# SyncE holds four loads back behind the first context, and seven tile norms move into the even rounds

## The chip, the cores and the metric

One core of a Trainium2 chip runs one launch of the kernel. The metric is the time of that launch on the device in microseconds (us). The engines are TensorE (PE, with its weight loads as PEld), VectorE (DVE), ScalarE (ACT), GpSimd (POOL) and SyncE (SP), which here only issues DMAs. Each runs its own instructions in order and waits on semaphores for the others.

## The reference

A small perceiver of six residual layers over `x` (16 sequences of 64 rows, 256 wide) and a context (16 x 1601 rows, 192 wide). The change touches only the first layer:

```python
x = x + _L0_xattn_ref(_layernorm(x), ctx_768, wq, bq, wk, bk, wv, bv, wo, bo)
# _L0_xattn_ref: 16 heads of 16
q = (x @ wq + bq)                      # from the normed x
k, v = (y @ wk + bk), (y @ wv + bv)    # from the context
attn = softmax(einsum('bqhd,bkhd->bhqk', q, k) / sqrt(16))
out = einsum('bhqk,bkhd->bqhd', attn, v) @ wo + bo
```

Self-attention, a feed-forward layer, a second cross-attention, a test-time-trained memory and a mixture of experts follow.

## The kernel before

The first layer is the function `latents`. `x` lies as 8 tiles of 128 rows (`c.x`, each tile two sequences). An item n (0 to 31) is one sequence and one half of the heads; b = n // 2 is the sequence. After a lead-in the layer runs rounds r from -3 to 64, two rounds an item. Each engine has its own function (`pe`, `dve`, `act`, `pool`, `sp`) which walks through the same rounds, so the place of a step in each of these lists is the order in which that engine does it.

What the rounds hold, as far as it is needed here:
- Context loads: `sp` loads the first context in two parts, columns 0 to 400 and the rest, three DMAs each; then `wq`, `wo`, the other seven tiles of `x`, the second context (`load_raw(1)`), the output bias `biasb` and two stores of zeros. `load_raw(2)` then waits for the split of the first context. ACT and POOL split every context into high and low parts (`split`, L689 and L690, L783 and L787; for the first context POOL L837 and DVE L648).
- PE, in a round from 0 on: `scores` of one group (4 banks of PSUM), `look_at` of one group (4 banks), `values` of the round before (1 bank), then a second `scores` (4 banks) and a second `look_at` (4 banks); after that in odd rounds the turn of the maxima, and in both kinds `keys` (L410 to L414) and `vals` (L425 to L429) for what comes next. Banks are given out by a counter modulo 8 (`at`), so the last of the four banks of the second `scores` is the one that the first `look_at` filled first, and the first three banks of the second `look_at` are the next three of it. PE waits for each (`take`) until it has been emptied.
- DVE empties the look banks with `maxima`, four TENSOR_REDUCE (L574) a group. In an even round it does: maxima, an add (L600), maxima, the maximum (L582 to L587), `invert` (L609), an add (L603). In an odd one: maxima, two adds (L603), maxima, `gather` (L617, L621), an add (L603).
- POOL in an even round: an add (L808), `blockdiag` (L797), two adds (L813), `scale` (L825, L828), then a split (L783, L787). In an odd round: adds (L813), a sum (L818), a split.
- The layer norm of a tile has three steps: `moments` on DVE (L169, L171), `root_pool` on POOL (L178 to L189, six tiny instructions that each wait for the one before), `norm_tile` on DVE (L196), which waits for the root. Tile 0 is done in the lead-in. `norms = {-3: (1, 2, 3), -2: (4, 5), -1: (6, 7)}` says in which round the others are: `moments` at the start of DVE's round, `root_pool` on POOL after `scale` and ahead of the split, `norm_tile` at the end of DVE's round, ahead of the next round's maxima. PE turns tile t (`turn_h`) in round 2t - 1.
- POOL adds the output bias to all of `c.x` in one instruction (L857) in round -1. DVE needs it in `project`, first in round 10.
- `dve_ahead` (L1091 to L1094) is a little work for the next layer, at the end of DVE's round 2.

Of the kernel before, what the change touches and what calls it, by code (L numbers as in the profile page):

```python
# [9 lines left out]
ALU = mybir.AluOpType  # L10
# [4 lines left out]
NT = 8  # L15
# [184 lines left out]
def latents(c, first, then):  # L200
# [30 lines left out]
    x0 = "x0"  # L231
# [6 lines left out]
    seen, m_made, m_turned, m_out = c.sig("seen"), c.sig("m_made"), c.sig("m_turned"), c.sig("m_out")  # L238
    added_d, added_p, totals = c.sig("added_d"), c.sig("added_p"), c.sig("totals")
    padded, in_ctx, in_rest = c.sig("padded"), (c.in_ctx, c.sig("in_ctx_odd")), c.sig("in_ctx_rest")  # L240
    norms = {-3: (1, 2, 3), -2: (4, 5), -1: (6, 7)}

    def probs(n, s):

# [108 lines left out]
    def sp(e, w):  # L353
        x = d["x"].rearrange("(t b) n c -> (b n) t c", b=2)
        for k in ("wk", "wv"):
            e.dma_start(W[k], d["x0_" + k]).then_inc(c.in_wkv.at(k, 16), 16)
        e.dma_start(c.x[:, 0, :], x[:, 0, :]).then_inc(c.in_wkv.at("x", 16), 16)
        for k, arrived in ((slice(0, 400), in_ctx[0]), (slice(400, NK), in_rest)):
            e.dma_start(raw1[0][:, k], d["ctxT"][0, 0:128, k]).then_inc(arrived.at(None, 16), 16)
            e.dma_start(raw2[0][0:64, k], d["ctxT"][0, 128:192, k]).then_inc(arrived.at(None, 16), 16)  # L360
            e.dma_start(raw2[0][64:128, k], d["ctxT"][0, 128:192, k]).then_inc(arrived.at((x0, 0), 16), 16)
            if k.start == 0:
                e.dma_start(c.ident[:, :], d["ident"]).then_inc(c.in_const.at("ident", 16), 16)
                e.dma_start(c.small[:, 0:c.n_const], d["small"]).then_inc(c.in_const.at("small", 16), 16)
        for k in ("wq", "wo"):
            e.dma_start(W[k], d["x0_" + k]).then_inc(c.in_wqo.at(k, 16), 16)
        e.dma_start(c.x[:, 1:NT, :], x[:, 1:NT, :]).then_inc(c.in_x.at("x", 16), 16)

        def load_raw(b):
            if b >= 2:  # L370
                w.wait_ge(*c.split_hi((x0, b - 2, 3)))
                w.wait_ge(*c.split_lo((x0, b - 2, 3)))
            if b == 2:
                w.wait_ge(*c.dv(("first low", 3)))
            e.dma_start(raw1[b % 2], d["ctxT"][b, 0:128, :]).then_inc(in_ctx[b % 2].at(None, 16), 16)
            e.dma_start(raw2[b % 2][0:64, :], d["ctxT"][b, 128:192, :]).then_inc(in_ctx[b % 2].at(None, 16), 16)
            e.dma_start(raw2[b % 2][64:128, :], d["ctxT"][b, 128:192, :]).then_inc(in_ctx[b % 2].at((x0, b), 16), 16)

        load_raw(1)
        e.dma_start(c.biasb[:, :], d["x0_bo"].partition_broadcast(128)).then_inc(c.in_bias[0].at("in", 16), 16)  # L380
        w.wait_ge(*c.po("zeros"))
        for v in (c.xs_d, c.ys_d):
            e.dma_start(v[1024:1152, :], c.zeros[:, :]).then_inc(c.zeroed.at("rows", 16), 16)
        for b in range(2, NB):
            load_raw(b)

    def pe(e, w):
# [53 lines left out]

        def queries(tile):
            w.wait_ge(*c.hT_act((x0, tile)))
            w.wait_ge(*c.in_wqo("wo"))
            bk = take("q", tile)
            for g in range(2):
                a = mm(e, ps[:, bk, 128 * g:128 * g + 128],
                       [(W["wq"][:, k, 128 * g:128 * g + 128], hT[:, k, 128 * tile:128 * tile + 128]) for k in range(2)])
            a.then_inc(c.q_made.at((x0, tile)), 1)
            emptied[bk] = c.q_out((x0, tile))  # L450
# [69 lines left out]

        def project(tile):
            w.wait_ge(*c.o_norm((x0, 4 * tile + 3)))
            bk = take("o", tile)
            mm(e, ps[:, bk, 0:256], [(aT[:, g, :], W["wo"][:, g, :]) for g in range(2)]).then_inc(c.projected.at((x0, tile)), 1)
            emptied[bk] = c.x_new((x0, tile))
# [34 lines left out]
    def dve(e, w):  # L560
# [61 lines left out]

        def project(tile):
            w.wait_ge(*c.projected((x0, tile)))
            w.wait_ge(*c.biased(x0))
            e.tensor_tensor(c.x[:, tile, :], ps[:, at("o", tile), 0:256], c.x[:, tile, :], ALU.add).then_inc(c.x_new.at((x0, tile)), 1)
            w.wait_ge(*c.x_new((x0, tile)))
            moments(c, e, w, x0, tile)
# [150 lines left out]
    def pool(e, w):  # L779
        def split(b, i):  # L780
            k = slice(400 * i, 400 * i + 400 + (i == 3))
            w.wait_ge(*c.split_hi((x0, b, i, 1)))
            e.tensor_tensor(c1l[b % 2][:, k], raw1[b % 2][:, k], c1h[b % 2][:, k], ALU.subtract).then_inc(c.po.at(), 1)  # L783
            w.wait_ge(*c.split_hi((x0, b, i)))
            w.wait_ge(*c.po.now())
            lo = c2[b % 2][64:128, k]
            e.tensor_tensor(lo, raw2[b % 2][64:128, k], lo, ALU.subtract).then_inc(c.split_lo.at((x0, b, i)), 1)  # L787
            w.wait_ge(*c.split_lo((x0, b, i)))

        def blockdiag(n):  # L790
            b, g = n // 2, n % 2
            w.wait_ge(*c.q_out((x0, b // 2)))
            w.wait_ge(*c.in_const("small"))
            if n >= 3:
                w.wait_ge(*c.scored((x0, n - 3, 3)))
            q = qT[b // 2 % 2][:, g, 64 * (b % 2):64 * (b % 2) + 64]
            e.tensor_tensor(qd[n % 3], q.unsqueeze(1).broadcast_to([128, 2, 64]), c.parq.unsqueeze(2).broadcast_to([128, 2, 64]),  # L797
                            ALU.mult).then_inc(c.q_diag.at((x0, n)), 1)

        def add(n, s):  # L800
            if (n, s) > (N - 2, 1):
                return
            v = probs(n, s)
            w.wait_ge(*c.exp_a((x0, n, s, 3)))
            if s == 0:
                if n:
                    w.wait_ge(*totals(n - 1))
                e.tensor_tensor(sums_p, v[:, :, 256:384], v[:, :, 384:512], ALU.add).then_inc(added_p.at((n, s)), 1)  # L808
            else:
                for t in range(share(n, s), GN[s]):  # L810
                    k = 128 if G0[s] + t < 12 else KL
                    w.wait_ge(*added_p.now())
                    e.tensor_tensor(sums_p[0:k], sums_p[0:k], v[0:k, :, 128 * t:128 * t + 128], ALU.add).then_inc(added_p.at((n, s)), 1)  # L813

        def add_both(n):
            w.wait_ge(*added_d((n, 3)))
            w.wait_ge(*added_p((n, 3)))
            e.tensor_tensor(sums_p, sums_p, sums_d, ALU.add).then_inc(added_p.at((n, "all")), 1)  # L818

        def scale(n):  # L820

            w.wait_ge(*c.o_out((x0, 2 * n + 1)))
            if n:
                w.wait_ge(*c.o_norm((x0, n - 1)))
            e.tensor_tensor(oS, va, vb[:, 0:128], ALU.add).then_inc(c.po.at(), 1)  # L825
            w.wait_ge(*c.po.now())
            w.wait_ge(*c.dv(("inverted", n)))
            e.tensor_tensor(oS, oS, rS, ALU.mult).then_inc(c.po.at(("scaled", n)), 1)  # L828

        e.memset(c.half, -0.5).then_inc(c.po.at("half"), 1)  # L830
        e.memset(c.eps, 1e-5).then_inc(c.po.at("eps"), 1)
        e.memset(c.zeros[:, :], 0.0).then_inc(c.po.at("zeros"), 1)
        root_pool(c, e, w, "in", 0)
        for i in range(4):
            k = slice(400 * i, 400 * i + 400 + (i == 3))
            w.wait_ge(*c.split_hi((x0, 0, i, 1)))
            e.tensor_tensor(c1l[0][:, k], raw1[0][:, k], c1h[0][:, k], ALU.subtract).then_inc(c.split_lo.at((x0, 0, i)), 1)  # L837
        blockdiag(0)
        for r in range(FIRST, LAST + 1):
            for use in groups(r)[:1]:  # L840
                add(*use)
            if r % 2 == 0 and 1 <= (r + 4) // 2 < N:
                blockdiag((r + 4) // 2)
            for use in groups(r)[1:]:
                add(*use)
                if r % 2 and r // 2 < N - 2:
                    add_both(r // 2)
            if r >= 2 and r % 2 == 0:
                scale(r // 2 - 1)
            for t in norms.get(r, ()):  # L850
                root_pool(c, e, w, "in", t)
            if splits(r) is not None:
                split(*splits(r))
            if r == -1:
                w.wait_ge(*c.in_bias[0]("in"))
                w.wait_ge(*c.normed(("in", NT - 1)))
                e.tensor_tensor(c.x[:, :, :], c.x[:, :, :], c.biasb[:, :].unsqueeze(1).broadcast_to([128, NT, D]),  # L857
                                ALU.add).then_inc(c.biased.at(x0), 1)
            then.pool(e, w, r)

    def ended(w):
# [2315 lines left out]
```

## Time and profile before

| | |
|---|---|
| runs of the kernel, median (lowest, highest) | 1898.99 us (1897.92, 1899.85), 3 runs |
| the profiled execution, its own time | 1897.95 us |
| its span | 1895.9 us |
| PE, DVE, ACT, POOL busy | 96%, 68%, 50%, 48% of the span |
| the first of 40 slices (0 to 47 us) | PE 6 tenths; the next slices 9 |
| the share of PE in the chain that ended last | 77%; DVE 10%, ACT 6%, DMA 2% |

A slice of the span is 47.4 us. The page shows an engine's busy share in tenths; PE has 9 (90% or more) in nearly all slices after the first, so PE sets the pace nearly everywhere and the holes in it lie in the first 50 us. The page's times are in us from the span's start, and the round that is called r = 4 below runs on PE from about 85.7 to 95.9 us.

### The profile page before, as it was taken

The page shows a single profiled execution, that of the slowest core. Times are in us where ns is not written, and L with a number is a line of the kernel's source. Part 1 is how long each engine was busy: PE and PEld are TensorE (multiplying, and loading weights), DVE is VectorE, ACT ScalarE, POOL GpSimd, SP SyncE. Part 2 cuts the span into 40 slices and gives each one's busy share as a digit, 9 for nine tenths or more (in the row PEclk, how much of TensorE's full clock was granted, in tenths as well). Part 3 has the DMA queues.
Part 4 walks back from the last instruction along what each step waited for, and adds up shares of the span by engine and source line. Part 5 has one row for each costly group of instructions (what it writes and reads, how often), then busy time and mean ns, then how long its engine had stood idle before and what let it go on. Part 6 is the DMA issues. An engine that isn't in the chain of part 4 may idle for free.

```text
span 1895.9 us, 44166 instructions
## 1 busy us (share of the span) xinstructions
PE 1810.9 (96%) x17738; PEld 1532.8 (81%) x17738; DVE 1287.3 (68%) x2720; ACT 943.0 (50%) x2049; POOL 908.8 (48%) x1169
## 2 busy tenths in 40 slices
PE   6999999999999998999999999999999999899998
PEld 5788888888878777889999999999999967656665
DVE  6888888888888976567666667666676746652222
ACT  3766666666667735444444444444444424512221
POOL 5877777777787436256333333333333214412322
PEclk9999999999999999999999999999999999999999
DMA  5121111121110110233222222232322024131110
GB/s 160 37 58 50 37 37 37 47 62 37 37 37 3 58 46 1 71 81 106 62 61 62 62 62 62 62 86 72 86 62 61 1 109 184 54 136 31 24 32 13
DMA packets 50745, 113.07 MB, mean 60 GB/s; under 512 B 4928, under 2 KB 37264, under 8 KB 49008
## 3 DMA queue, kind: packets, MB, share of 16 engines
q1 hardware_dynamic: 46128, 105.13, 18.8%
q0 software_dynamic: 4416, 5.12, 1.6%
q8 instruction: 143, 2.34, 0.5%
q14 instruction: 58, 0.48, 0.1%
HBM read 105.78 MB, written 5.37 MB: 59 GB/s over the span
## 4 chain that ended last, share of the span: by engine, by line
PE 77%; DVE 10%; ACT 6%; issue 3%; DMA 2%; POOL 1%; SPq 0%; POOLq 0%; DVEq 0%; ACTq 0%
PE ps L164 8%; PE ps L104 7%; PE ps L2623 6%; PE ps L500 5%; PE ps L481 5%; PE ps L1687 4%; PE ps L458 4%; PE ps L2647 3%; PE ps L475 3%; PE ps L1688 2%; PE ps L410 2%; DVE arena L1799 2%; DMA wsb<-in_ctxT 2%; DVE arenaR L1793 2%; PE ps L1674 2%
## 5 line engine op out<-in xcount | busy, mean ns | idle before, releaser
L574 DVE TENSOR_REDUCE arena<-ps 128x1 f32<-128x400 f32 (+1 forms) x512 | 257.3, 564 | 82.8 <-PE ps L458 82.5
L729 ACT ACTIVATE arena<-ps 128x384 f32<-128x384 f32 (+1 forms) x512 | 223.3, 524 | 94.2 <-PE ps L481 93.8
L1687 PE MATMUL ps<-arenaR 128*128 128x386 f32 x768 | 241.9, 372 | 1.1 <-DVE arenaR L1793 1.1
L813 POOL TENSOR_TENSOR arena<-arena 128x512 f32<-128x512 f32 (+1 forms) x152 | 196.6, 1293 | 81.3 <-ACT arena L729 74.1
L1903 ACT CAST arenaR<-ps 128x512 fp32r<-128x512 f32 (+1 forms) x256 | 116.7, 508 | 201.9 <-PE ps L164 201.1
L1688 PE MATMUL ps<-arenaR 128*128 128x194 f32 x768 | 193.9, 252 | 0.0
L1793 DVE TENSOR_TENSOR arenaR<-ps,arenaR 128x512 fp32r<-128x512 f32 (+1 forms) x256 | 138.8, 584 | 28.6 <-ACT arenaR L1903 28.6
L1688 PEld LDWEIGHTS ps<-arenaR 128*128 128x128 f32 x768 | 146.9, 191 | 0.0
L1928 ACT ACTIVATE wsb<-ps,arena 128x1200 f32<-128x1200 f32 x64 | 81.0, 1265 | 131.5 <-DVE arena L1852 131.5
L1687 PEld LDWEIGHTS ps<-arenaR 128*128 128x128 f32 x768 | 144.9, 189 | 1.4 <-DVE arenaR L1793 1.4
L1799 DVE TENSOR_REDUCE arena<-ps 128x1 f32<-128x400 f32 (+1 forms) x256 | 137.0, 566 | 0.6 <-PE ps L1677 0.6
L2623 PE MATMUL ps<-gu,rest 128*128 x276 | 129.0, 604 | 2.8 <-issue 2.8
L500 PEld LDWEIGHTS ps<-arena 128*32 128x32 f32 (+1 forms) x3328 | 87.0, 110 | 42.6 <-ACT arena L729 42.4
L164 PE MATMUL ps<-ident,wsb 128*128 128x128 f32 (+1 forms) x832 | 112.3, 273 | 4.2 <-ACT wsb L1930 2.2
L1943 POOL TENSOR_TENSOR arenaR<-wsb,arenaR 128x400 fp32r<-128x400 f32 (+1 forms) x32 | 29.0, 907 | 182.0 <-ACT arenaR L1875 181.9
L481 PE MATMUL ps<-arena 32*128 32x128 f32 x3328 | 114.1, 269 | 0.0
L481 PEld LDWEIGHTS ps<-arena 32*128 32x128 f32 x3328 | 112.4, 186 | 1.2
L1943 POOL TENSOR_TENSOR xA<-wsb,xA 128x400 fp32r<-128x400 f32 (+1 forms) x32 | 29.3, 916 | 174.8 <-ACT xA L1875 174.5
L458 PE MATMUL ps<-arena 32*128 32x400 f32 (+1 forms) x1024 | 111.7, 499 | 0.3 <-DVE arena L568 0.3
L500 PE MATMUL ps<-arena 128*32 128x128 f32 (+1 forms) x3328 | 104.2, 274 | 3.9 <-ACT arena L729 0.4
L2927 POOL DMA_INDIRECT out_x<-rest,irest x23 | 36.3, 1580 | 146.2 <-DVE rest L2742 146.2
L2880 ACT ACTIVATE rest<-ps 128x256 f32<-128x256 f32 x69 | 26.5, 384 | 159.5 <-PE ps L2623 159.5
(370 smaller groups left out, 4962.6 us busy)
## 6 DMA issues: line engine op xcount, KB each, us to landing
wsb<-in_ctx SPq DMA_DIRECT2D x16, 1152.0 KB
wsb<-in_ctxT SPq DMA_DIRECT2D x16, 800.5 KB, 4.9
wsb<-in_ctxT SPq DMA_DIRECT2D x32, 400.2 KB, 7.4
gu<-in_m_gu SPq DMA_DIRECT2D x8, 1536.0 KB, 19.2
arena<-in_ctxT SPq DMA_DIRECT2D x15, 800.5 KB, 5.2
arena<-in_ctxT SPq DMA_DIRECT2D x30, 400.2 KB, 7.4
dn<-in_m_dn SPq DMA_DIRECT2D x8, 768.0 KB, 11.4
wsb<-in_f_w SPq DMA_DIRECT2D x2, 1024.0 KB, 5.9
```

The costliest lines, as they stand in the source:

```text
L164: return e.transpose(out, v, self.ident[0:k, 0:k])
L458: e.matmul(ps[:, bk, 0:real], flat(qd[n % 3])[r, :], K[n % 2][r, k.start:k.start + real], start=True, stop=True).then_inc(seen.at((n, i)), 1)
L481: a = e.matmul(ps[:, use[u], 128 * t:128 * t + 128], K[n % 2][r, k], flat(qd[n % 3])[r, :], start=False, stop=(t == T - 1))
L500: a = e.matmul(ps[32 * u:32 * u + 32, bk, 0:128], V[b % 2][0:rows, k, f + 32 * u:f + 32 * u + 32], probs(n, s)[0:rows, u, 128 * t:128 * t ...
L574: e.tensor_reduce(mx4[n % 2][:, u, i:i + 1], ps[:, at("look", n, i, u), 0:400 + (i == 3)], AX.X, ALU.max).then_inc(c.maxed.at((n, i, u)), 1)
L729: e.activation(v[:, u, 0:128 * GN[s]], ps[:, at("st", n, s, u), 0:128 * GN[s]], ACT.Exp).then_inc(c.exp_a.at((x0, n, s, u)), 1)
L813: e.tensor_tensor(sums_p[0:k], sums_p[0:k], v[0:k, :, 128 * t:128 * t + 128], ALU.add).then_inc(added_p.at((n, s)), 1)
L1687: e.matmul(o, PTh[:, t, :], v[:, t, 0:386], start=(t == 0), stop=False)
L1688: e.matmul(o[:, 0:194], PTl[:, t, :], v[:, t, 0:194], start=False, stop=False)
L1793: e.tensor_tensor(lo, ps[0:k, 4 + g % 2, 0:u], hi, ALU.subtract).then_inc(c.p_lo.at((x1, n, g)), 1)
L1799: e.tensor_reduce(mx4[n % 2][:, i:i + 1], ps[:, i, 0:400 + (i == 3)], AX.X, ALU.max).then_inc(c.dv.at(), 1)
L2623: p = e.matmul(ps[:, f, :], XT[i % 2][:, k, :], gu[:, bass.ds(off[i, 0] + (1536 * k + 512 * f), 512)], start=(k == 0), stop=(k == 1))
```

## The change

Three edits, all in the first layer:
- The loads: `wq` is issued ahead of the rest of the first context. Then SP waits until that rest has landed, and only after that issues `wo`, the other tiles of `x`, the second context, `biasb` and the stores. `queries` waits for `wq` alone; `project` on PE gets a wait for `wo` and `x`.
- The norms: each of the tiles 1 to 7 has its own even round, tile t in round 2t - 2, so tiles 1 to 7 lie in rounds 0, 2, 4, 6, 8, 10 and 12. Nothing of a norm is left in rounds -3 to -1.
- The bias: POOL adds it to one tile at a time, at the end of its even rounds (tile t in round 2t), in place of one instruction of 2048 columns in round -1.

```diff
-    norms = {-3: (1, 2, 3), -2: (4, 5), -1: (6, 7)}
+    norms = {2 * t - 2: (t,) for t in range(1, NT)}
...
         for k, arrived in ((slice(0, 400), in_ctx[0]), (slice(400, NK), in_rest)):
+            if k.start:
+                e.dma_start(W["wq"], d["x0_wq"]).then_inc(c.in_wqo.at("wq", 16), 16)
             e.dma_start(raw1[0][:, k], d["ctxT"][0, 0:128, k]).then_inc(arrived.at(None, 16), 16)
...
-        for k in ("wq", "wo"):
-            e.dma_start(W[k], d["x0_" + k]).then_inc(c.in_wqo.at(k, 16), 16)
+        w.wait_ge(*in_rest((x0, 0)))
+        e.dma_start(W["wo"], d["x0_wo"]).then_inc(c.in_x.at("wo", 16), 16)
         e.dma_start(c.x[:, 1:NT, :], x[:, 1:NT, :]).then_inc(c.in_x.at("x", 16), 16)
...
         def queries(tile):
-            w.wait_ge(*c.in_wqo("wo"))
+            w.wait_ge(*c.in_wqo("wq"))
...
         def project(tile):
             w.wait_ge(*c.o_norm((x0, 4 * tile + 3)))
+            w.wait_ge(*c.in_x("x"))
...
         def project(tile):
-            w.wait_ge(*c.biased(x0))
+            w.wait_ge(*c.biased((x0, tile)))
...
-            if r == -1:
+            if turns_h(r - 1) is not None or r == 0:
+                t = turns_h(r - 1) or 0
                 w.wait_ge(*c.in_bias[0]("in"))
-                w.wait_ge(*c.normed(("in", NT - 1)))
-                e.tensor_tensor(c.x[:, :, :], c.x[:, :, :], c.biasb[:, :].unsqueeze(1).broadcast_to([128, NT, D]),
-                                ALU.add).then_inc(c.biased.at(x0), 1)
+                w.wait_ge(*c.normed(("in", t)))
+                e.tensor_tensor(c.x[:, t, :], c.x[:, t, :], c.biasb[:, :], ALU.add).then_inc(c.biased.at((x0, t)), 1)
```

## Rows read from the trace of the kernel before

**Rows 1.** Waits of PE, 50 to 600 us: total, times, longest.
```profile
PE ps L475 <- ACT arena L729: 1.7, 1, 1.7
```
**Rows 2.** Timeline of ACT and PE, start of the context's rest: start, duration, count, [idle before].
```profile
13.69 0.52 ACT L689 CAST arenaR<-arena 128x400 fp32r<-128x400 f32 x1 [6.16 <-DMA arena<-in_ctxT]
...
15.91 0.67 PE L410 MATMUL ps<-arenaR 128*128 128x400 f32 x1 [3.15 <-DVE arenaR L648]
```
**Rows 3.** DVE timeline, lead-in: the norms of round -3; the statistics of one tile.
```profile
29.68 2.46 DVE L196 TENSOR_SCALAR h<-x,small 128x256 f32<-128x256 f32 x3
...
38.22 0.42 DVE L169 BATCH_NORM_STATS2 small<-x 128x6 f32<-128x256 f32 x1
```
**Rows 4.** PE timeline, keys and vals of round -2, and those of round 0.
```profile
33.74 0.70 PE L410 MATMUL ps<-arenaR 128*128 128x400 f32 x1 [2.97 <-DVE arena L574]
...
37.24 0.41 PE L425 MATMUL ps<-arenaR 128*128 128x256 f32 x1
...
39.37 0.34 PE L425 MATMUL ps<-arenaR 128*128 128x256 f32 x1
...
51.49 0.42 PE L410 MATMUL ps<-arenaR 128*128 128x400 f32 x1
...
53.37 0.28 PE L425 MATMUL ps<-arenaR 128*128 128x256 f32 x1
...
54.56 0.28 PE L425 MATMUL ps<-arenaR 128*128 128x256 f32 x1
```
**Rows 5.** Windows: stretch, PE, PEld, DVE, ACT, POOL busy, granted clock, DMA share, GB/s.
```profile
34.00:36.00 2.00, 2.00 (x7) 1.99 (x8) 2.00 (x5) 0.19 (x1) 1.57 (x6) 0.50 0.02 4
```
**Rows 6.** DMA issues: size, us from issue to landing (issued at 5.91 and 6.55).
```profile
arena<-in_ctxT SPq DMA_DIRECT2D x1, 300.2 KB, 7.8
...
arena<-in_x_wq SPq DMA_DIRECT2D x1, 256.0 KB, 6.7
```
**Rows 7.** DMA view, 4.92 to 13.67 us: all that was moved.
```profile
DMA packets 1258, 2.29 MB, mean 262 GB/s; under 512 B 275, under 2 KB 752, under 8 KB 1258
```
**Rows 8.** POOL timeline: a split of the lead-in, first and last instruction of a root.
```profile
8.81 1.05 POOL L837 TENSOR_TENSOR arenaR<-arena,arenaR 128x400 fp32r<-128x400 f32 x1
...
32.78 0.22 POOL L178 TENSOR_SCALAR small<-small 128x1 f32<-128x1 f32 x1 [0.31 <-DVE small L171]
...
34.56 0.19 POOL L189 TENSOR_TENSOR small<-small 128x1 f32<-128x1 f32 x1
```
**Rows 9.** DVE timeline: the norm of tile 0, released by its root.
```profile
8.76 1.24 DVE L196 TENSOR_SCALAR h<-x,small 128x256 f32<-128x256 f32 x1 [1.57 <-POOL small L189]
```
**Rows 10.** Line 196, all: ns min/median/max, first and last start.
```profile
L196 DVE TENSOR_SCALAR h<-x,small x39: 381/405/1242, 8.8 to 1650.1; 128x256 f32<-128x256 f32 x39
```
**Rows 11.** POOL timeline: the split right behind `scale`, rounds 2 and 4.
```profile
77.46 1.03 POOL L783 TENSOR_TENSOR arenaR<-arena,arenaR 128x400 fp32r<-128x400 f32 x1
...
96.97 1.04 POOL L783 TENSOR_TENSOR arenaR<-arena,arenaR 128x401 fp32r<-128x401 f32 x1
```
**Rows 12.** DVE timeline: end of round 2, first maxima of rounds 3 and 5.
```profile
77.11 0.41 DVE L1091 TENSOR_SCALAR small<-small 128x8 f32<-128x8 f32 x1
...
78.44 2.00 DVE L574 TENSOR_REDUCE arena<-ps 128x1 f32<-128x400 f32 x4
...
97.83 2.02 DVE L574 TENSOR_REDUCE arena<-ps 128x1 f32<-128x400 f32 x4 [1.12 <-PE ps L458]
```
**Rows 13.** PE timeline: the second look of rounds 1, 3 and 5.
```profile
60.27 0.84 PE L458 MATMUL ps<-arena 32*128 32x400 f32 x8
...
80.76 0.85 PE L458 MATMUL ps<-arena 32*128 32x400 f32 x8
...
100.31 0.84 PE L458 MATMUL ps<-arena 32*128 32x400 f32 x8
```
**Rows 14.** ACT and DVE timeline, round 0: the second group's exponentials; maxima of round 4.
```profile
50.85 1.64 ACT L729 ACTIVATE arena<-ps 128x384 f32<-128x384 f32 x4 [1.38 <-PE ps L481]
...
87.97 2.02 DVE L574 TENSOR_REDUCE arena<-ps 128x1 f32<-128x400 f32 x4 [1.33 <-PE ps L458]
```

## The prediction, made before the changed kernel ran

> **What bounds the kernel now.** I read the page first: PE has nine tenths or more in nearly all slices and six in the first, so PE's time is the kernel's time, and what is open to gain lies ahead of 50 us. Then the waits of PE from 50 to 600 us: the longest, and nearly the only one, is 1.7 us, once, on ACT [rows 1]. So in the rounds PE never waits for DVE or POOL now. Whatever makes it wait there is lost in full, and DVE and POOL have no value there beyond being in time. The timelines of the lead-in show two holes. From the first, ACT sits idle until the rest of the first context lands, starts at 13.69, and PE follows at 15.91 after 3.15 idle [rows 2]. The second: DVE runs three norms, 2.46 us, and the moments of two more tiles before it turns to the maxima, and PE waits 2.97 us for the first bank they empty [rows 3, 4]. Behind that hole the granted clock is 0.50, the 1.2 GHz level of the two [rows 5], and the ten keys matmuls take 37.24 - 33.74 = 3.50 us and ten vals matmuls 39.37 - 37.24 = 2.13 us, against 53.37 - 51.49 = 1.88 and 54.56 - 53.37 = 1.19 us in round 0 [rows 4].
>
> **The norms leave the lead-in: a gain.** DVE goes from the maxima of round -3, which end at 29.7, straight to those of round -2. Their first ends about 0.6 later, before PE has finished the look at 30.8, so PE's 2.97 us go. With no hole ahead of it the clock should stay up: (3.50 - 1.88) + (2.13 - 1.19) = 2.56 us. Together 5.5 us. I see nothing late next: the roots no longer hold POOL's splits back either, and ACT copies within a microsecond of PE. The ends: 3.0 us if the clock falls all the same, 5.5 us if not; I take 5.5. The stretch from the look of round -1 to the first scores keeps its length, since DVE was waiting for PE at its start.
>
> **The loads: a small gain or a loss.** Between 4.92 us, when the first piece of the rest is issued, and its landing at 13.67 the queue moved 2.29 MB [rows 7]. The rest is 1.23 MB. From the sizes, about 0.26 MB ahead of it was still under way at 4.92; so 0.8 MB belonged to loads issued later. Now `wq`, 0.26 MB, is ahead of the rest in any case, and 0.54 MB can be held off: 0.54 / 0.262 = 2.0 us earlier at best. At worst the later loads never slowed the rest, and `wq` costs its own 0.26 / 0.262 = 1.0 us, or up to 2 us if the slowest part of the queue moves at half that rate. What speaks for sharing: `wq`, issued at 6.55, landed 6.7 later at 13.25, before the last piece of the rest, issued at 5.91, which took 7.8 [rows 6]. I take 0.7 us gained, with ends of -2.0 and +2.0. Behind SP's wait stand `wo`, `x`, the second context, `biasb`, the stores and `load_raw(2)`. The first user of `x` is DVE in round 0, after 40 us, and the second context is needed by ACT at about 25 us, with 1.6 MB of it and 1.2 MB ahead: from 13.0 at 262 GB/s that is 10.7 us, so 24 us. That cover is thin, about a microsecond; what is over is a wait of ACT ahead of its copies of vals. The new wait of PE's `project` for `x` is met long before round 9, and `wq` lands before the keys are done; both cost nothing.
>
> The Trainium skill (DMA: Bandwidth & Descriptors, Queues, rings and completion order) says that on each DMA engine descriptors are consumed in ring order, so on one issuing queue later loads would not start ahead of the rest and holding them would bring nothing, with `wq` a loss. The trace agrees only in part, by the 13.25 against 13.67 above. By the rule the sum below would be 1.7 to 2.7 us higher.
>
> **The norms enter the even rounds: the large term.** Moments, 0.42 us of statistics [rows 3] and a small aggregate, come at the start of DVE's round, where it is idle 1.33 us before round 4's maxima [rows 14]: nothing. The norm at the end is another matter, because it waits for a root that POOL starts only after `scale`, and because DVE's next round stands behind it. In round 4 POOL is free of `scale` at 96.97, where the split starts [rows 11]. The root's six instructions run from 32.78 to 34.56 + 0.19, 1.97 us [rows 8]. The norm alone takes 0.405 us (the median of line 196), but 1.24 us for tile 0 [rows 9, 10], which started beside the POOL split of 8.81 to 9.86 and ended just behind it [rows 8]. In the new order the same pair meets: the split starts right behind the root. So I take 1.24 us. Then four maxima, 2.02 us [rows 12], and PE's second look of round 5 needs the bank of the last of them: 96.97 + 1.97 + 1.24 + 2.02 = 102.20, where PE wants it at 100.31 [rows 13]. PE stands 1.89 us. The first part of it falls on the second scores just ahead, whose fourth bank is the first look's first, emptied 1.5 us before the last. Rounds 6, 8, 10 and 12 repeat this pattern with the same distances within 0.05 us: five rounds, 5 x 1.9 = 9.5 us.
>
> Round 2 also has the three little instructions of the next layer behind the norm, 78.44 - 77.11 = 1.33 us [rows 12]: 77.46 + 1.97 + 1.24 + 1.33 + 2.02 = 84.02 against PE at 80.76 [rows 11, 13], 3.3 us. In round 0 there is no `scale`: POOL's adds follow the exponentials that end at 52.49 [rows 14], two adds of 1.3 us, then 1.97 + 1.24 + 2.02, so 60.3 against 60.27 [rows 13]: 0.1 us. Sum 9.5 + 3.3 + 0.1 = 12.9 us. The bounds: with a norm of 0.405 us it is 0.83 less in each of six rounds, 12.9 - 5.1 = 7.8 us. Above, DVE and POOL come out of a norm round some 0.5 us late even against the delayed PE, and the short round pair 7 and 8 leaves least room to recover; that may add 0.5 to 2 us.
>
> **The bias.** One tile is an eighth of the columns, about 0.6 us on POOL behind the split in eight even rounds, ahead of odd rounds in which POOL waits for ACT. The single long one goes from round 0's start, where PE did not wait for it. Both at nothing; if POOL's cover is gone, part of the 0.5 to 2 us above.
>
> **Sum.** 1897.95 - 5.5 - 0.7 + 12.9 = 1904.65 us, against the profiled execution's own time (span 1895.9 and 2.05 us around it). That execution is 1.0 us below the median of the runs shown, so for a median I say 1905.3 us.
>
> **Rivals.**
> - The full stalls, and the clock drops once more. Round 3's hole is about 2.7 us in one piece and half a microsecond after it; 2.97 us came ahead of the low clock at 34 us [rows 4, 5]. It would cost what it cost there, 2.6 us: 1907.9 us. Against it: the single 1.7 us wait left the clock up.
> - The norm isn't held up by POOL: 7.8 us instead of 12.9: 1900.2 us. For it, most of the 39 norms take 0.405 us; against it, those ran beside no split that started at the same moment.
> - The waits are absorbed: the root is early or PE has a slack that I don't see, and only round 2 costs, 0 to 2 us. Then the lead-in's gain stands: 1892.7 us up to 1894. It decides from a root that ends by 96.7 in round 4's terms, 2.2 us sooner than its place on POOL allows; little speaks for it.
> - The hold of the loads misses: the rest lands as before or later and the second context late for ACT. 1.7 to 2.7 us onto whichever of the above, so 1907 to 1908 us on the forecast.
> - Lateness grows from round to round, as DVE and POOL don't recover: up to 1912 us.
>
> **How the numbers follow.** Forecast as summed (1903 to 1907) 0.38; with the clock drop, late loads or growth (1907 to 1912) 0.30; norm not held up (1898 to 1903) 0.20; absorbed (1891 to 1896) 0.10; beyond all, 0.02. The range of 8 in 10 drops the absorbed case and the top of the growth: 1898.5 to 1911.5. A measurement of this kernel can tell about 0.2%, 3.8 us, from no change. Slower by more than that, above 1902.8: the first two cases and a little of the third, 0.69. Within: most of the third and the edge of the fourth, 0.20. Faster, below 1895.2: 0.11.
>
> **What would show it.** Right if the waits of PE between 60 and 190 us hold six new ones on DVE L574, at L475 and L458, of 1.4 and 0.5 us, the largest in round 3; if line 196 shows about 1.24 us seven times; if the maxima start behind L196 with no idle; if the hole of 2.97 at 33.7 and the 0.50 clock behind it are gone. The loads are judged by the start of the second L689 against 13.69. I am wrong if PE shows no wait in the rounds, which would make the bank argument false, or if norms start earlier than two microseconds after `scale`.

## The result, and the profile after

The changed kernel takes 1907.16 us in the median of 14 runs (1896.38 to 1912.95), the kernel before, in 14 runs, 1898.45 us. The ratio is 1.0042 with a 95% interval of 1.0026 to 1.0058: slower by 8 us, 5 to 11. The forecast was 1905.3 us, "slower" with a chance of 0.69. The profiled execution took 1908.24 us, its span is 1906.1 us, 10.2 us longer than before. Three later executions of the kernel before (2022 to 2220 us, at a mean granted clock of 0.75 to 0.85) were slow throughout and stand outside of every number given here.

The waits of TensorE between 50 and 610 us, over the same rounds as [rows 1] (total, times, longest). L477, L460 and L577 are the scores, the look and the maxima, L475, L458 and L574 before:

```profile
PE ps L477 <- DVE arena L577: 10.8, 8, 2.5
```

Eight waits on the maxima are new, 10.8 us in all: six of 1.5 to 2.5 us and two small ones, 0.2 and 0.4. The wait on ScalarE of [rows 1] is not gone; it has only moved ahead of 50 us (1.67 us, at 43.25).

The lead-in on TensorE's timeline, the same instructions as in [rows 4] (L412 is the first keys matmul, L427 the first of vals):

```profile
28.20 1.73 PE L460 MATMUL ps<-arena 32*128 32x400 f32 x16
...
29.93 0.45 PE L412 MATMUL ps<-arenaR 128*128 128x400 f32 x1
...
31.85 0.28 PE L427 MATMUL ps<-arenaR 128*128 128x256 f32 x1
```

The keys of round -2 follow the look without a hole and take the time of the higher clock: 31.85 - 29.93 = 1.92 us for ten, where before ten took 3.50. The 2.97 us and the low clock behind them are gone.

Round 4, on GpSimd, VectorE and TensorE: what answers to [rows 8, 9 and 11 to 13].

```profile
94.70 0.22 POOL L178 TENSOR_SCALAR small<-small 128x1 f32<-128x1 f32 x1
...
96.48 0.19 POOL L189 TENSOR_TENSOR small<-small 128x1 f32<-128x1 f32 x1
96.75 1.03 POOL L786 TENSOR_TENSOR arenaR<-arena,arenaR 128x401 fp32r<-128x401 f32 x1
```

```profile
96.70 1.22 DVE L196 TENSOR_SCALAR h<-x,small 128x256 f32<-128x256 f32 x1 [2.40 <-POOL small L189]
97.85 2.00 DVE L577 TENSOR_REDUCE arena<-ps 128x1 f32<-128x400 f32 x4
```

```profile
98.56 0.45 PE L477 MATMUL ps<-arenaR 32*128 32x384 f32 x4 [1.52 <-DVE arena L577]
...
99.47 1.37 PE L460 MATMUL ps<-arena 32*128 32x400 f32 x8
```

The root takes 94.70 to 96.67, as one did in the lead-in. VectorE has stood 2.40 us for it. The norm starts in the same moment as GpSimd's split and takes 1.22 us. The maxima come at 97.85 with no idle ahead of them, where before they waited for TensorE, and TensorE's second scores stand 1.52 us; the look after it takes 1.37 instead of 0.84 us, and its second half waits for the maxima once more (its weight load at 99.90, 0.19 us on L577).

One mark a round shows where the time goes: the start of the values matmuls (L500 before, L502 after), in us.

| values of round | 1 | 2 | 3 | 4 | 5 | 6 | 8 | 10 | 12 | 14 | 61 |
|---|---|---|---|---|---|---|---|---|---|---|---|
| before | 57.66 | 68.44 | 78.15 | 87.95 | 97.69 | 108.47 | 127.09 | 148.47 | 167.98 | 188.51 | 652.03 |
| after | 51.31 | 62.38 | 72.08 | 85.55 | 95.30 | 107.69 | 128.55 | 151.55 | 173.03 | 195.20 | 658.88 |
| difference | -6.35 | -6.06 | -6.07 | -2.40 | -2.39 | -0.78 | +1.46 | +3.08 | +5.05 | +6.69 | +6.85 |

The lead-in gives 6.35 us, seven steps take 13.0 back, and from round 14 to near the end of the layer (round 61) nothing more is lost. The other 3.4 us of the span's 10.2 arise behind the first layer, which the change does not touch. The windows of the self-attention show where (columns as in [rows 5]); first before, then after:

```profile
720.00:730.00 10.00, 7.27 (x100) 6.42 (x93) 6.68 (x9) 5.29 (x9) 9.83 (x7) 0.83 0.01 2
730.00:740.00 10.00, 9.89 (x116) 8.89 (x116) 6.30 (x11) 5.41 (x10) 9.60 (x8) 1.00 0.01 2
```

```profile
720.00:730.00 10.00, 5.61 (x60) 4.68 (x59) 7.95 (x8) 7.47 (x13) 4.88 (x4) 0.91 0.00 0
730.00:740.00 10.00, 10.00 (x86) 9.22 (x84) 5.27 (x7) 3.52 (x6) 9.68 (x7) 0.50 0.01 2
740.00:750.00 10.00, 10.00 (x56) 9.06 (x56) 3.49 (x6) 2.28 (x4) 8.55 (x6) 0.50 0.00 0
```

The granted clock stays at its lower level for over 20 us after, for a few before. By 794 us that had put the kernel 14.3 us behind (the last L999, 780.1, against the last L1002, 794.4), of which 4 came back later. Whether that is the change or chance is asked below.

### The profile page after: what moved, and what is told of

It is laid out like the page before. It is cut to its first block, busy times and chain, and to the rows that moved or that the text cites. A ratio compares the mean times of both kernels' runs of the same rounds, so it can differ in the third digit from the quotient of the medians.

```text
span 1906.1 us, 44188 instructions
## 1 busy us (share of the span) xinstructions
PE 1818.5 (95%) x17738; PEld 1540.2 (81%) x17738; DVE 1284.7 (67%) x2720; ACT 943.1 (49%) x2049; POOL 914.6 (48%) x1176
## 4 chain that ended last, share of the span: by engine, by line
PE 73%; DVE 12%; ACT 6%; issue 4%; DMA 2%; POOL 1%; SPq 0%; POOLq 0%; DVEq 0%; ACTq 0%
PE ps L164 8%; PE ps L104 7%; PE ps L2626 6%; PE ps L1690 4%; PE ps L483 4%; PE ps L502 4%; PE ps L460 4%; PE ps L2650 3%; PE ps L477 2%; DVE arena L577 2%; PE ps L1691 2%; DVE arena L1802 2%; DMA wsb<-in_ctxT 2%; DVE arenaR L1796 2%; PE ps L1677 2%
## 5 line engine op out<-in xcount | busy, mean ns | idle before, releaser
L577 DVE TENSOR_REDUCE arena<-ps 128x1 f32<-128x400 f32 (+1 forms) x512 | 257.6, 565 | 75.7 <-PE ps L460 75.3
L502 PEld LDWEIGHTS ps<-arena 128*32 128x32 f32 (+1 forms) x3328 | 87.0, 110 | 42.6 <-ACT arena L732 42.3
L460 PE MATMUL ps<-arena 32*128 32x400 f32 (+1 forms) x1024 | 116.1, 503 | 0.3 <-DVE arena L571 0.3
L502 PE MATMUL ps<-arena 128*32 128x128 f32 (+1 forms) x3328 | 104.2, 274 | 3.8 <-ACT arena L732 0.4
L606 DVE TENSOR_TENSOR arena<-arena 128x512 f32<-128x512 f32 x132 | 105.9, 802 | 1.4
L164 PEld LDWEIGHTS ps<-ident,wsb 128*128 128x128 f32 (+1 forms) x832 | 98.4, 141 | 8.8 <-DVE arenaR L1796 2.9
```

What stands on the lines that cost most here:

```text
L164: return e.transpose(out, v, self.ident[0:k, 0:k])
L460: e.matmul(ps[:, bk, 0:real], flat(qd[n % 3])[r, :], K[n % 2][r, k.start:k.start + real], start=True, stop=True).then_inc(seen.at((n, i)), 1)
L502: a = e.matmul(ps[32 * u:32 * u + 32, bk, 0:128], V[b % 2][0:rows, k, f + 32 * u:f + 32 * u + 32], probs(n, s)[0:rows, u, 128 * t:128 * t ...
L577: e.tensor_reduce(mx4[n % 2][:, u, i:i + 1], ps[:, at("look", n, i, u), 0:400 + (i == 3)], AX.X, ALU.max).then_inc(c.maxed.at((n, i, u)), 1)
```

## The experiments

All marks are the starts of the values matmuls of rounds 1 and 14; what lies between them, 130.85 us before and 143.89 after, is the price of the norms in the rounds. "Rest" is the start of ScalarE's second L689, when the rest of the first context has landed.

**The loads as they were.** An edit of the changed kernel: the `wq` line ahead of the rest, SyncE's wait and the wait on `wq` alone are undone.

```diff
-        w.wait_ge(*in_rest((x0, 0)))
-        e.dma_start(W["wo"], d["x0_wo"]).then_inc(c.in_x.at("wo", 16), 16)
+        for k in ("wq", "wo"):
+            e.dma_start(W[k], d["x0_" + k]).then_inc(c.in_wqo.at(k, 16), 16)
```

> The changed kernel with its loads as they were: wq and wo behind the rest of the first context, no wait on SyncE. Marks: the second L692 on ScalarE (rest landed; 13.69 us before, 12.75 with the change) and the values of rounds 1 and 14 on TensorE (57.66 and 188.51 before, 51.31 and 195.20 with the change). My theory, the hold lets the rest land 0.9 us earlier in spite of wq ahead of it: rest at 13.7, round 1 at 52.2, round 14 at 196.1. Rival one, the queue runs in order and the 0.9 us are chance from run to run: rest anywhere from 12.5 to 14, no step between the kernels. Rival two, wq ahead of the rest costs 1 us, so without both the rest lands at 11.8 and round 1 is at 50.4.

Measured: 1899.26 us; rest at 13.14, round 1 at 52.01, round 14 at 195.85. Between the first theory (13.7) and the changed kernel (12.75): this one profile tells nothing apart, except that rival two's 11.8 did not come. The price in the rounds is the same, 143.84.

**wq ahead, but no wait.**

```diff
-        w.wait_ge(*in_rest((x0, 0)))
```

> The changed kernel without SyncE's wait, but with wq still ahead of the rest of the first context. If the later loads share the queue with the rest, the rest lands at 13.7 + 1.0 = 14.7 us (wq's 0.26 MB at 262 GB/s) and round 1 is at 53.2. If the queue runs in order, the wait does nothing: rest at 12.75 as with the change, round 1 at 51.3.

Measured: 1901.85 us; rest at 13.42, round 1 at 52.25, in the rounds 143.82. Neither number came: in this one profile `wq` ahead of the rest did not cost its microsecond.

**The hold alone, norms and bias as before.**

```diff
-    norms = {2 * t - 2: (t,) for t in range(1, NT)}
+    norms = {-3: (1, 2, 3), -2: (4, 5), -1: (6, 7)}
```

(and the bias in one instruction again)

> The kernel before with the new order of loads and SyncE's wait alone; norms and bias as before. My theory: the rest at 12.75 us, the gain of 0.9 us goes through: round 1 at 56.7, round 14 at 187.6, no wait in the rounds. Rival: the moments of round -3 now wait for x, which is issued behind the wait, and eat the gain: round 1 at 57.7 or later, with DVE L169 waiting for a DMA.

Measured: 1893.87 us; rest at 14.71, round 1 at 57.96, round 14 at 188.82. The hold is in this kernel, and the rest landed a microsecond later than without it before. So the 0.94 us of the changed kernel's profile need not be the hold's. The rival's sign is absent: VectorE's moments of round -3 start at 24.48 with no wait on a DMA. In the rounds 130.86, as before.

**The bias a tile at a time, nothing else.**

```diff
-            if r == -1:
+            if turns_h(r - 1) is not None or r == 0:
```

> The kernel before with the bias added a tile at a time in rounds 0 to 14 and nothing else. My theory: no price and no gain on TensorE, round 1 at 57.7 and round 14 at 188.5, each within 0.2 us. Rival: the single bias instruction of 4.55 us held DVE's add of round 0 and with it the maxima, so its going gives up to 1.7 us; or eight small ones ahead of POOL's adds cost 0.1 to 0.3 us each, so round 14 at 189.5 or later.

Measured: 1894.18 us; round 1 at 57.66, round 14 at 188.41, in the rounds 130.75. Without the long bias instruction VectorE's add of round 0 takes 1.42 us where it took 3.47, but TensorE did not wait for it before and gains nothing. The small instructions cost nothing either. The rest landed at 14.00 here with the very loads of the kernel before (13.69).

**The split waits for the norm.** An edit of the changed kernel in `pool`:

```diff
             for t in norms.get(r, ()):
                 root_pool(c, e, w, "in", t)
+                w.wait_ge(*c.normed(("in", t)))
             if splits(r) is not None:
```

> The changed kernel, where POOL starts the split behind a root only when DVE has done the norm that this root releases. Marks: values of round 1 and 14 on TensorE (51.31 and 195.20 with the change). My theory, the norm takes 1.22 us because POOL's split starts in the same moment: seven norms of 0.41 us, each of the six later stalls 0.8 us shorter, round 14 at 190.3, round 1 unchanged. Rival: the norm behind a root is slow by itself, or POOL's later split takes the gain back: line 196 still at 1.2 us seven times, round 14 at 195.2 or later.

Measured: 1903.68 us; round 1 at 52.72, round 14 at 194.24, in the rounds 141.52. VectorE's timeline, round 4:

```profile
97.69 0.41 DVE L196 TENSOR_SCALAR h<-x,small 128x256 f32<-128x256 f32 x1 [2.39 <-POOL small L189]
```

All seven norms took 0.41 us: it was the split that held them up. The direct waits on the maxima fell from 10.8 to 5.9 us; between 50 and 300 us:

```profile
PE ps L477 <- DVE arena L577: 5.9, 6, 1.9
```

Three waits are there that the changed kernel doesn't have between these times: L519 on GpSimd's L821 (0.3 us, at 129.34), L104 on VectorE's L624 (0.6, at 147.94) and L460 on VectorE's L571 (0.3, at 172.05).

But the rounds became only 2.4 us shorter, not 4.9. From round 5 to 6 it is the 0.8 us expected (11.58 against 12.39), from 9 to 10 it is 0.4 more than in the changed kernel. The collision moved instead of going. VectorE and GpSimd of round 3:

```profile
78.07 3.56 DVE L606 TENSOR_TENSOR arena<-arena 128x512 f32<-128x512 f32 x2
```

```profile
77.98 1.26 POOL L816 TENSOR_TENSOR arena<-arena 128x512 f32<-128x512 f32 x1
79.80 2.97 POOL L816 TENSOR_TENSOR arena<-arena 128x512 f32<-128x512 f32 x2 [0.56 <-ACT arena L732]
```

Two adds of VectorE that took 1.78 us in that round before (at 80.37) and 1.43 in the changed kernel (at 77.52), beside one add of GpSimd, now meet three and take 3.56. In rounds 5, 7, 9 and 11 it is a small instruction of the `gather` (L624) that takes 1.34 to 1.36 us beside GpSimd's adds, where it took 0.28 in the changed kernel. So VectorE gave back in its next round much of what it had gained at the norm, and the three new waits are places where TensorE felt it. Round 3 also had the lower clock, behind a hole of only 1.92 us, and for as long as the changed kernel: 3.4 us, by the windows (0.50 in 78 to 80 and 0.65 in 80 to 82 us, against 0.54 in 76 to 78 and 0.60 in 78 to 80). How much of the missing 2.5 us is which, this run doesn't separate.

**The three small instructions out of round 2.**

```diff
     def dve_ahead(e, w, r):
-        if r == 2:
+        if r == 1:
```

> The changed kernel with the next layer's three little DVE instructions at the end of round 1 in place of round 2. The change moved the values of round 4 from 2.4 us to round 3's distance: the pair of rounds 3 and 4 lost 3.7 us, the pairs behind it 1.6 to 2.2. My theory: the first pair is dearer by the 1.3 us (here 0.9) of these instructions and by the lower clock that follows the longer hole; without them it loses 1.6 to 2.0 us, the granted clock stays at 1.0 behind it, round 14 at 193.2. Rival: the first pair is dearer for its place, what POOL has queued there: round 14 at 195.2 and the same low clock at 76 us.

Measured: 1906.66 us; round 14 at 194.54 from 52.36, in the rounds 142.18, 1.71 us less than 143.89. From round 3 to 4 it is 11.77 us, against 13.47 in the changed kernel and 9.80 before: that pair now costs 1.97 like the others. The windows of that place, the changed kernel first, then this one:

```profile
76.00:78.00 2.00, 1.70 (x28) 1.73 (x32) 2.00 (x5) 0.00 (x0) 1.67 (x2) 0.54 0.03 8
```

```profile
76.00:78.00 2.00, 1.59 (x34) 1.44 (x36) 2.00 (x5) 0.35 (x1) 1.92 (x3) 1.00 0.03 8
```

A hole of 2.48 us ahead of 76.3 us was followed by the lower clock, one of 1.55 us in this run was not.

**The root first on GpSimd.** An edit of the changed kernel: the loop over `root_pool` goes from behind `scale` to the start of the round.

```diff
         for r in range(FIRST, LAST + 1):
+            for t in norms.get(r, ()):
+                root_pool(c, e, w, "in", t)
             for use in groups(r)[:1]:
...
-            for t in norms.get(r, ()):
-                root_pool(c, e, w, "in", t)
             if splits(r) is not None:
```

> The changed kernel with root_pool at the start of POOL's even round, ahead of its adds, in place of behind scale; the norm stays at the end of DVE's round. My theory: the stalls come from the late root alone. POOL has 0.4 to 2 us idle at that place, the norm finds its root done, and only round 2, where the next layer's three instructions follow, may keep 0 to 1 us: round 14 at 182.2 to 183.2, no wait on DVE L577 of over 0.3 us elsewhere. Rival: two microseconds more on POOL ahead of its adds come out elsewhere, as waits of TensorE's L519 on POOL or of ScalarE's exponentials on the adds: round 14 at 185 or later.

Measured: 1890.60 us; round 1 at 51.63, round 14 at 182.49: in the rounds 130.86, the kernel before's 130.85. Between 50 and 300 us TensorE waits for nothing. VectorE's norm of round 2 comes right behind its add, with no wait:

```profile
70.54 0.62 DVE L606 TENSOR_TENSOR arena<-arena 128x512 f32<-128x512 f32 x1
71.09 0.54 DVE L196 TENSOR_SCALAR h<-x,small 128x256 f32<-128x256 f32 x1
...
129.63 1.35 DVE L196 TENSOR_SCALAR h<-x,small 128x256 f32<-128x256 f32 x1
```

The same norms in the same rounds, the same bias and loads, and all of the 13.0 us are gone. The late root is the cause: one of the norms (129.63) was even slower than the 1.22 us of the changed kernel, and TensorE did not wait.

**The root first, and the three instructions in round 1.** Both edits together.

> Root at the start of POOL's even round and the next layer's three instructions in round 1, both on top of the change. My theory: no stall is left in rounds 1 to 14; round 1 at 51.3, round 14 at 182.2, the time 6.3 us below the kernel before: about 1892, a ratio of 0.9967. Rival: the lead-in's gain is given back by POOL's added 2 us in each even round: ratio 1.000 or above.

Measured: 1891.95 us in the median of 12 runs, the kernel before beside it 1895.89; ratio 0.9988 with an interval of 0.9970 to 1.0007. In the rounds 130.83, round 1 at 51.95. The expected 0.9967 is just outside the interval. The first layer's end comes 5.6 us earlier than before (the values of round 61 at 646.46 against 652.03), and the whole shows 2.3, with zero still possible.

**The same with the old loads.**

> The version with the root first and the three instructions in round 1, with the loads as they were before the change. Over six profiles with the hold and four without, the rest of the first context started being split at 12.8 to 14.7 and at 13.1 to 14.0 us, so I expect no step: the values of round 1 at 51.5 to 52.5 us, of round 14 at 182.3 to 183.3, ratio 0.997 to 0.999. If the hold is worth its 0.9 us after all, round 1 lies at 52.9 or later.

Measured: 1896.10 us in the median of 12 runs, the kernel before beside it 1898.11; ratio 0.9986 (0.9971 to 1.0002). Rest at 13.96, round 1 at 52.45, round 14 at 183.27. By the ratio it is the kernel with the hold.

**The kernel before once more.**

> The kernel before, unchanged, to see what its own executions differ by. Theory: most of the scatter comes from how long the granted clock stays low in the self-attention after 720 us (5 to 25 us long in the profiles so far). Then the runs spread over some 10 us, the mean granted clock of the core falls as the time rises, and the values of rounds 1 and 14 stay at 57.7 and 188.5 within 0.5 us. If instead the first layer itself scatters, these two marks move by microseconds.

Measured: rest at 14.18, round 1 at 58.12, round 14 at 188.95; its runs lie between 1892.16 and 1905.50 us, ratio 0.9997 (0.9977 to 1.0016). The times go with the granted clock: 1892.16 us at a mean of 0.994, 1899.26 at 0.989, 1905.50 at 0.985. The self-attention, in its windows:

```profile
720.00:730.00 10.00, 7.77 (x84) 7.11 (x88) 5.99 (x7) 4.22 (x7) 9.83 (x8) 0.57 0.01 2
730.00:740.00 10.00, 10.00 (x93) 9.27 (x85) 3.99 (x7) 4.45 (x7) 9.59 (x8) 0.58 0.00 0
```

In the first profile of this same kernel these stood at 0.83 and 1.00: some 3 us at the lower level there, 17 here. The first layer does not scatter so: its two marks moved by half a microsecond, what lies between them by 0.02.

## Why the prediction was right

**The norms leave the lead-in: right, and its size is that of one execution.** Predicted 5.5 us of gain. From the start of the look of round -3 to that of round -1 TensorE takes 11.67 us in the profile on which this was worked out and 6.12 in the changed kernel's, 5.55 less: the hole of 2.97 and 2.57 of clock. But the other three profiles with the norms in the lead-in take 10.68, 10.57 and 10.45 us there (the other seven with the norms in the rounds 6.12 to 6.14). They have the same hole of 2.98, but their lower clock lasts about half as long (in the windows 0.97 and 0.68 over 30 to 40 us in hold_only, 0.77 and 0.55 in the kernel before) and costs 1.3 to 1.6 us. So the gain is 4.3 to 5.6 us, and that the changed kernel's profile met the 5.5 is in part luck. Between the means of round 1 (57.85 in four profiles, 52.08 in eight) lie 5.8 us, of which 0.9 are an earlier landing of the rest.

**The loads: the size was wrong, within its ends.** Predicted 0.7 us with ends of -2.0 and +2.0. With the wait the rest was there at 12.75, 14.71, 13.87, 12.89, 13.15 and 13.00 us, without it at 13.69, 13.14, 13.42, 14.00, 13.96 and 14.18. The means are 13.4 and 13.7; one kernel's own two profiles differ by 0.5 (13.69, 14.18). By the means the wait is worth 0.3 us; the scatter leaves room for nothing and for the 0.7 predicted, and what of it reaches round 1 can't be told. What failed is the working behind the 2.0 us: it took what others moved in that time as what they cost the rest. The DMA view from 4.92 us to the landing, of the changed kernel, is to be held against [rows 7]:

```profile
DMA packets 856, 1.77 MB, mean 226 GB/s; under 512 B 252, under 2 KB 472, under 8 KB 856
```

The other five profiles with the wait show 1.78 to 1.83 MB at 187 to 223 GB/s, the six without it 2.09 to 2.36 MB at 245 to 275. The wait did keep about half a MB away, but the queue then moved less in a microsecond, and the rest came hardly sooner. The 0.94 us in the changed kernel's own profile look like the term, but hold_only's 14.71 with the same loads shows that they may well be chance. `wq` ahead of the rest had no price that shows, and the thin cover of the second context held: ScalarE waited 0.16 us for it at 24.66 in the changed kernel and 0.53 at 25.37 in root_first. The Trainium skill's rule that each ring is consumed in order (DMA: Bandwidth & Descriptors, Queues, rings and completion order) would have a wait on SyncE bring nothing and `wq` cost something; the twelve landings don't contradict the first and show nothing of the second.

**The norms in the even rounds: right, and the large term.** Predicted 12.9 us, measured 13.0. By rounds: 0.1 predicted for round 0 and 0.3 found; 3.3 and 3.7 for round 2; 1.9 each for rounds 4, 6, 8, 10 and 12, found 1.6, 2.2, 1.6, 2.0 and 1.6, so the lateness did not grow from round to round. In round 5 TensorE starts the turn behind its late look 1.9 us late, as worked out, and has regained 0.3 of it by the next values. That 3.3 met 3.7 in round 2's pair is in part luck: the three small instructions took 0.9 us and not 1.33, and the lower clock, which the sum left out, made up for it. The mechanism is shown piece by piece: the late root by root_first, the 1.22 us beside the split by split_after_norm, the bank by the rows of L477. 

**The bounds.** The lower bound with a norm of 0.405 us, 7.8 us, was too low: the run with such norms lost 10.7 us in the rounds. I took 0.83 us off six rounds as if VectorE kept what it saved. Behind the norms of rounds 4, 6 and 12 it did (0.8, 1.1 and 0.9 us less). Behind that of round 2 the gain was 0.1 us, and between the values of rounds 8 and 12 TensorE lost 0.9 us more than in the changed kernel; there lie the three new waits.

**The clock drop, a rival with its own price: it happened, at a lower price.** The hole in round 3 was 2.48 us and the clock fell behind it. But the pair was dearer than the others by 1.7 us only, and 0.9 of these are the three small instructions (74.66 to 75.59 in the changed kernel). So the lower clock cost at most 0.8 us, not 2.6. It was a short stretch, 3.4 us where the one in the lead-in had 6.8; that TensorE had to wait for banks in part of it may be another reason, which no run shows.

**The sum.** 1904.65 us and the 1.0 us up to the median make 1905.7; the recorded 1905.3 is 0.4 short of its own sum. 1897.95 + 6.7 was meant for a whole kernel whose rest stays as it is. The first layer's end moved by 6.85 us. The median moved by 8.7, within the interval of 5 to 11. The 3.4 us more in the profiled execution lie in the self-attention. Behind the first layer's last values the ten other profiles take 1237.7 to 1246.3 us, the kernel before 1243.9 and the changed one 1247.2: a scatter as large as the effect. The clock alone doesn't explain the difference between 6.85 and 8.7. Its mean is 0.992 over the changed kernel's 14 runs and 0.990 to 0.991 over the 49 runs of the kernel before that have it on record, beside later kernels. At 0.988 the medians are 1909.6 and 1901.0 us (six runs each), at 0.993 to 0.995 they are 1903.3 and 1891.7 (four and ten): 9 to 12 us at an equal clock. Since those runs were not made beside the changed kernel's, this is a hint and no more. What stays open is where behind the first layer 2 us or more are lost, if they are, and whether an earlier or later start has to do with it. The two best kernels gave 5.6 and 4.8 us in the first layer and 2.3 and 2.7 us by their ratios, whose intervals hold anything from 5.7 to -1.3 us; the runs don't decide whether anything was given back.

## What to carry to other kernels

A norm of three steps over two engines costs the engine that takes the last step not its own 0.4 us but the wait for the middle step, and that is set by where the other engine has it in its order. When work is moved out of a stage where it is seen waiting into one that has room by its busy share, read the distance in each engine's order from the release to the next thing that the pace-setting engine needs: here 5.2 us of chain had 3.3 us of room, in every norm round but the first. Moving the middle step to the start of its engine's round kept the whole gain in the first layer and cost nothing there; in the whole kernel the gain isn't clear of zero.

## What the runs showed of the hardware

- A VectorE norm of 0.41 us took 1.22 to 1.25 us seven times of seven in the changed kernel, where a GpSimd split starts within 0.06 us of it. Taking that collision away moved it: norms at 0.41 us, yet two adds at 3.56 instead of 1.43 us in the next round.
- A hole of 2.48 us on TensorE was followed by the lower clock (0.54 over 2 us) in the changed kernel, as was one of 1.92 us in split_after_norm by 0.50, while the five of 1.5 to 1.6 us further on in the changed kernel left it at 1.00.
- Behind one and the same hole of 2.97 to 2.98 us in the lead-in the clock was low for some 7 us in one execution of the kernel before and 3 in another, and in the self-attention for 3 us in the first and 17 in the second. Most of the 13 us by which the runs of one kernel differ goes with the mean granted clock (0.994 to 0.985).
- A microsecond of a transfer's landing is not a kernel's property in this lead-in: one and the same order of loads gave 13.1 to 14.2 us in five profiles, the order with the wait 12.8 to 14.7 in six.
- The queue did not carry the rest faster when it had less else to carry: 1.77 MB at 226 GB/s with the wait, 2.29 MB at 262 without it.
